# Adjacency tiles that serve two sweeps: a six-sweep graph kernel with the flat sweeps in alternating row order

## The reference

```
L0: inv_deg = 1/(adj.sum(1) + beta); x = LN(x + inv_deg * (adj @ x + beta*x) @ kernel + bias)
L1: h = relu(adj @ (x @ W1) + b1); h = relu(adj @ (h @ W2) + b2); h = relu(adj @ (h @ W3) + b3)
    x = LN(x + relu(h + x))          # W1: 128 x 20, W2: 20 x 20, W3: 20 x 128
L2: fc = x @ W + b; d = 1/(sqrt(adj.sum(1)) + 1e-8); x = LN(x + (adj * d[:,None] * d[None,:]) @ fc)
L3: S = (x@W_l) @ (x@W_r).T; x = LN(x + adj @ x + gamma * softmax(S) @ x @ W_h @ W_g)
```

## Time and profile before

| what | us |
|---|---|
| median of 3 runs | 1440.37 |
| profiled execution, its own time | 1445.9 |
| its span | 1444.3 |
| PE, DVE, ACT, GpSimd busy | 1367.3, 899.6, 709.5, 254.9 |
| copy of the last sum of sweeps 0, 3, 4, 5 starts at | 265.17, 634.50, 825.42, 1011.34 |
| HBM read | 342.65 MB |

### The profile page before, as it was taken

One profiled execution on the slowest core, in us unless ns is written; L12 is line 12 of the kernel. 1 busy time (PEld: TensorE's weight loads), 2 busy tenths in 40 slices (PEclk: granted clock), 3 DMA queues, 4 the chain that ended last, 5 costly groups with the idle time before them and its releaser, 6 DMA issues.

```text
span 1444.3 us, 17225 instructions
## 1 busy us (share of the span) xinstructions
PE 1367.3 (95%) x5879; PEld 798.7 (55%) x5879; DVE 899.6 (62%) x1194; ACT 709.5 (49%) x883; POOL 254.9 (18%) x167
## 2 busy tenths in 40 slices
PE   6999999888898999999999999999899999999987
PEld 2555555321222222247777778888667777767754
DVE  4676777300000013368888898888788888888885
ACT  1110011111101111257777787776787887887786
POOL 0111111000000000101010000000533333345345
PEclk9999999999999999999999999999999999999999
DMA  9866677699999999998999999997000000000000
GB/s 361 332 260 233 253 277 271 248 391 406 407 404 408 408 401 408 390 362 301 313 323 309 338 324 365 354 386 271 0 0 1 0 1 0 1 1 29 0 1 29
DMA packets 103455, 345.69 MB, mean 239 GB/s; under 512 B 11610, under 2 KB 13274, under 8 KB 103386
## 3 DMA queue, kind: packets, MB, share of 16 engines
q1 hardware_dynamic: 101136, 343.98, 63.3%
q10 hardware_dynamic: 2250, 0.82, 0.2%
HBM read 342.65 MB, written 2.10 MB: 239 GB/s over the span
## 4 chain that ended last, share of the span: by engine, by line
PE 75%; DMA 15%; DVE 5%; ACT 3%; issue 1%; POOL 0%; SPq 0%; DVEq 0%; ACTq 0%
DMA raw<-in_adj_s 15%; PE acc L1104 11%; PE acc L1140 9%; PE acc L1202 7%; PE acc L1197 7%; PE acc L1198 7%; PE acc L1297 6%; PE acc L1124 4%; PE acc L1227 2%; PE acc L1287 2%; PE acc L1291 2%; PE acc L1288 2%; DVE t_lo L829 2%; PE e L1252 2%; PE e L1254 2%; PE e L1253 2%
## 5 line engine op out<-in xcount | busy, mean ns | idle before, releaser
L829 DVE TENSOR_TENSOR t_lo<-raw,t_hi 128x1024 fp32r<-128x1024 f32 x240 | 292.1, 1248 | 42.4 <-ACT t_hi L589 36.9
L589 ACT ACTIVATE t_hi<-raw 128x1024 fp32r<-128x1024 f32 x240 | 251.5, 1058 | 60.4 <-PE acc L1202 58.9
L1197 PE MATMUL acc<-t_hi,st_hi 128*128 128x512 f32 x480 | 202.3, 421 | 2.9 <-DVE st_lo L734 2.9
L500 POOL TENSOR_TENSOR ring_lo<-ring,p_hi 128x1024 fp32r<-128x1024 f32 x64 | 155.6, 2430 | 220.2 <-ACT p_hi L647 220.1
L1198 PE MATMUL acc<-t_hi,st_lo 128*128 128x512 f32 x480 | 187.5, 391 | 0.0
L1140 PE MATMUL acc<-raw,h_a 128*20 128x512 f32 x736 | 161.8, 599 | 25.8 <-DMA raw<-in_adj_s 25.5
L1104 PE MATMUL acc<-raw,x 128*128 128x512 f32 x384 | 174.0, 608 | 11.2 <-DMA raw<-in_adj_s 11.2
L760 DVE TENSOR_TENSOR xs<-e,bias 128x512 f32<-128x512 f32 x8 | 5.5, 690 | 272.0 <-PE e L1020 272.0
L534 ACT ACTIVATE at<-acc 128x512 f32<-128x512 f32 x48 | 28.7, 598 | 266.4 <-PE acc L1140 181.9
L913 DVE TENSOR_TENSOR ring<-ring,e 128x1024 f32<-128x1024 f32 x128 | 154.1, 1212 | 0.7 <-PE e L1267 0.6
L1202 PE MATMUL acc<-t_lo,st_hi 128*128 128x512 f32 x480 | 149.9, 393 | 0.7 <-DVE t_lo L829 0.7
(11 more groups left out here) (189 smaller groups left out, 2062.1 us busy)
## 6 DMA issues: line engine op xcount, KB each, us to landing
raw<-in_adj_s SPq DMA_DIRECT2D x600, 512.0 KB, 6.9
resident<-in_adj_s SPq DMA_DIRECT2D x16, 512.0 KB, 7.7
raw<-in_adj_s SPq DMA_DIRECT2D x24, 256.0 KB, 7.7
kept_t<-in_adj_s SPq DMA_DIRECT2D x8, 512.0 KB, 5.8
x<-in_x SPq DMA_DIRECT2D x4, 512.0 KB, 8.4
kept_s<-in_adj_s SPq DMA_DIRECT2D x8, 256.0 KB, 6.1
kept_v<-in_adj_s SPq DMA_DIRECT2D x8, 256.0 KB, 6.5
kept_l<-in_adj_s SPq DMA_DIRECT2D x8, 256.0 KB, 9.0
```

Source lines behind the costliest of these rows:

```text
L500: nc.gpsimd.tensor_tensor(ring_lo[:, n % RING, :], slot(n), p_hi[:, m % 2, :].bitcast(F32), ALU.subtract).then_inc(pl_done, 1)
L589: nc.scalar.activation(t_hi[:, (par * wide_tiles(s) + g) % HL, :], raw[:, k, :], ACT.Copy).then_inc(hi_done, 1)
L829: nc.vector.tensor_tensor(t_lo[:, k, :], raw[:, slot_no(s, c, g), :], t_hi[:, k, :].bitcast(F32), ALU.subtract).then_inc(lo_done, 1)
L1197: mm(a[:, :], block_of(st_hi, b), hi[:, m], start=(b == 0), stop=False)
```

## The change

The flat sweeps are planned by a list of items (tile of row chunk c, column chunk d, half h). Sweeps 1 and 3 take the row chunks backwards (7 to 0). When tile (c, d) is on chip for sweep s and the `h` of sweep s+1 for column chunk d is already known, its product for sweep s+1 is added too, in a second accumulator `ahead` (the banks of `rs01`), and the tile is not needed in sweep s+1. ACT stores the partial sum (`store_ahead`, in `sums`), and in sweep s+1 DVE, not ACT, takes the chunk's sum and adds the stored one (`evacuate_narrow`). The distance in rows from which a tile is joined is `lag`: 1 in sweep 0, 2 in sweeps 1 and 2, and 1 in the rows c > 3 of sweep 2, which lets these last four chunks also join the column chunk next to them.

```
+ORDER = (tuple(range(NC)), tuple(reversed(range(NC))), tuple(range(NC)), tuple(reversed(range(NC))))
+LATE = 1
+KEPT = tuple((c, c + 1) if c + 1 < NC else (c, c - 1) for c in range(NC))
+def lag(s, c):
+    return 1 if s == 0 or s == 2 and c > 3 else 2
+def joined(s, c, d):
+    return s < 3 and used(s, c, d) and ORDER[s].index(c) - ORDER[s].index(d) >= lag(s, c)
+def used(s, c, d):
+    return s == 0 or not joined(s - 1, c, d)
+def held(s, c, d):
+    return d in KEPT[c] and not (s == 0 and c == LATE)
...
+def order_of(s, c):
+    mine = [d for d in range(NC) if used(s, c, d)]
+    if s == 0:
+        last = [d for d in mine if c > 0 and d in KEPT[c] and d != c - 1] + [d for d in mine if d == c - 1]
+    else:
+        last = [d for d in (c + 1, c - 1, c) if d in mine and d in KEPT[c]]
+        if s == 1:
+            mine.reverse()
+    return [d for d in mine if d not in last] + last
```

In sweep 0 (`first_sweep`) a joined column chunk gets its four narrow matmuls after its second tile; in `narrow_sweep` each joined tile has its own two blocks in two strips and the next sweep's two in the other two:

```
+                    if i.fused and i.h == 1:
+                        wait_h(pe, 0, i.d)
...
+                        for b in range(CB):
+                            t = tile_of(0, c, items[n - 1 + b // GB])
+                            m = mm(f[32 * b:32 * b + H, :], h_a[:, (i.d * CB + b) * H:(i.d * CB + b + 1) * H],
+                                   t[:, b % GB * CW:(b % GB + 1) * CW], start=(i.d == joint[0]),
+                                   stop=(i.d == joint[-1]))
...
+                    for j in range(GB):
+                        b, k = i.d * CB + i.h * GB + j, 32 * (2 * i.h + j)
+                        m = mm(a[k:k + H, :], h[:, b * H:(b + 1) * H], t[:, j * CW:(j + 1) * CW],
+                               start=(i.d == items[0].d), stop=(i.d == items[-1].d))
+                    if i.fused:
+                        for j in range(GB):
+                            b, k = i.d * CB + i.h * GB + j, 32 * (2 * (1 - i.h) + j)
+                            m = mm(f[k:k + H, :], h_next[:, b * H:(b + 1) * H], t[:, j * CW:(j + 1) * CW],
+                                   start=(i.d == joint[0]), stop=(i.d == joint[-1]))
```

```
+                    if n == (1 if r > 0 else -1):
+                        epilogue_1(ps, pr, pr % 2)
+                    if ps < 3 and (n == (min(4, len(items) - 1) if r > 0 else -1)):
+                        epilogue_2(ps, pr)
+                    if s == 3:
+                        for q in TURNED[r]:
+                            if n == (2 if q < r - 1 else 9):
+                                epilogue_3(3, q)
+                            if n == (4 if q < r - 1 else 12):
+                                epilogue_4(3, q)
```

with `TURNED[r]` the rows q whose turn belongs to row r: r - 2 for q up to 3, r - 1 for later ones. Before the first item of sweep 1 PE runs all of the last row's epilogue. On DVE a row of sweep 3 is, in order:

```
+                evacuate_narrow(ps, pr)
+                if ps == 3:
+                    residual_1(ps, pr)
+                    residual_2(ps, pr)
+                    statistics(ps, pr)
+                    scales(ps, pr)
+                    for q in TURNED[r]:
+                        laplacian_h(q)
+                    if r > 2:
+                        stationary_lo(S4, row(3, r - 3))
```

More of the change, by code:

```diff
@@ L23 @@
 NG = NB // GB
-RB = 4
 TW = GB * CW
@@ L62, with done, row, plan @@
 }
-def done(stage, s, c):
-    return c + (1 + NC * sum(q < s for q in STAGES[stage]))
+def done(stage, s, r):
+    return r + (1 + NC * sum(q < s for q in STAGES[stage]))
+ORDER = (tuple(range(NC)), tuple(reversed(range(NC))), tuple(range(NC)), tuple(reversed(range(NC))))
+LATE = 1
+KEPT = tuple((c, c + 1) if c + 1 < NC else (c, c - 1) for c in range(NC))
+Item = namedtuple("Item", "d h kept fused seq")
+def row(s, r):
+    return ORDER[s][r] if s in FLAT else r
+def lag(s, c):
[15 more added lines that the diff above has]
+    return [d for d in mine if d not in last] + last
+def plan():
+    items, seq = {}, 0
+    for s in FLAT:
+        for r, c in enumerate(ORDER[s]):
+            here = []
+            for d in order_of(s, c):
+                for h in range(CB // GB):
+                    streamed = not held(s, c, d)
+                    here.append(Item(d, h, not streamed, joined(s, c, d), seq if streamed else None))
+                    seq += streamed
+            items[s, r] = here
+    return items, seq
+ITEMS, T_WIDE = plan()
+STORES = [(s, r) for s in FLAT for r in range(NC) if any(i.fused for i in ITEMS[s, r])]
+def stored(s, c):
+    return STORES.index((s, ORDER[s].index(c))) + 1 if (s, ORDER[s].index(c)) in STORES else 0
+def same_bank(s, r):
+    return max((n + 1 for n, (q, t) in enumerate(STORES) if (q, t) < (s, r) and t % 2 == r % 2), default=0)
 def build(nc, adj_s, x_dram, beta_in, ident_in, comb_in, w, out):
@@ L392, in load_kept @@
             def load_kept(c):
[L393 to L407, removed]
-            def step(s, c, par):
[L410 to L422, removed]
+                if c > 2:
+                    sp.wait_ge(res_in, 64 * (c - 2))
@@ L423, in step @@
+            first_of_1 = min(i.seq for r in range(NC) for i in ITEMS[1, r] if not i.kept)
+            def step(s, c, par):
+                if s in FLAT:
+                    flat(s, c)
+                    return
+                for g in range(NG):
+                    wait_slot(sp, s, c, g)
                     k = slot_no(s, c, g)
[L424 removed]
+                    sp.dma_start(raw[:, k, :], tile(c, group_no(s, c, g))).then_inc(raw_in[k], 16)
@@ L534, in evacuate, with store_ahead @@
                 nc.scalar.activation(at[:, :], acc[par][:, :], ACT.Copy).then_inc(S["at"], 1)
+            def store_ahead(s, r):
+                if (s, r) not in STORES:
+                    return
+                act.wait_ge(pe_acc, s * NC + r + 1)
+                if s > 0:
+                    act.wait_ge(S["at"], done("at", s, r))
+                nc.scalar.activation(sums[:, row(s, r), :], ahead[r % 2], ACT.Copy).then_inc(sums_done, 1)
             def second(s, c):
```

542 lines of the change are left out of this document (293 added, 249 removed).

## The result

The changed kernel takes 1362.27 us (median of 4 runs, 1358.85 to 1367.14) against 1440.50 in the same set: ratio 0.946, interval 0.9425 to 0.9497. In a second set it was 1363.14 (0.9437 to 0.9476). The prediction was 1339 in a range of 1318 to 1372; the rival of longer chains stood at 1365. So the time lies in the stated range, but above the 1326 to 1355 that was given for the forecast itself, and nearest to the rival of longer chains, which had a chance of 0.17. The profiled execution took 1359.29 us with a span of 1357.5, and from here on it is compared with before's 1444.3.

A forecast was written before the change was run, and what follows sets the result against it. Sweeps 1 to 3 were taken to wait for adjacency tiles. Stages 297.2 + 237.6 + 189.2 + 185.9 + 433.0 = 1342.9 against a 1444.3 span, 101.4 less; from the 1440.4 median, 1339 us, range 1318 to 1372.

The forecast's parts named there:

- the rival of longer chains: Sweeps 1 to 3: longer hops in 24 rows, 14 us, slow PE in 12 rows, 12 us; 1365 us, chance 0.17.
- signs named for a wrong prediction: Joined tile over 1 us, joined column in sweep 0 over 1.3 us, or sweep 3 over 90 us.
- Price of a column on PE: Sweeps 1 and 2: a joined tile takes 0.86 us, an unjoined one 0.43; bounds for joined 0.86 and 3.44.
- both rivals with two accumulators: Joined tiles in sweeps 1 and 2: in pairs, 1418 us, chance 0.04; one after another, up to 1576 us, 0.03.
- Sweep 1: Starts with a 13.1 us chain, then PE is full; takes 81.6 us, before about 127.
- Sweep 3: Nothing joined; DVE's chain decides; PE ends at +74.5, with loading and low clock 79 us.
- Row 0: Sweep 0's first row: PE waits 7 us for bx, row ends at 45.8 instead of 44.8; bounds 40 and 48.
- Sweep 4: Later chunks 22.6 us each, PE 22.3 and DVE 21.9; whole sweep 189.2 us, before 190.9.
- Sweep 2: Starts with a 3.7 us chain, row 0 1.8, row 1 4.7; takes 77 us.
- near but under it: Sweep 2's loading: 46 tiles after +6.4 end at +68, within the sweep's 77 us.
- Sweep 4's first chunk: Takes 31 us from the end of sweep 3, waiting inside DVE for the w3 matmuls; bounds 28 and 35.
- Sweep 0: 28 joined columns at 1.1 us add 31 us on full PE; ends at 297.2, before 265.2.

The follow-up runs named there:

- the half loads: Changed kernel, but in sweep 3's rows 4 to 7 only the first column block of each streamed tile is loaded: 1361.54 us.
- Moving DVE's steps: Changed kernel with constants first, PE kept busy and lag 2 in sweep 2; DVE's epilogue steps one tile later in sweep 4's first chunk: 1347.97 us against 1345.64.
- PE kept busy: Changed kernel plus idle wide matmuls in PE's waits where sweeps 1, 2 and 3 begin: 1356.62 us, 6.5 less than the changed kernel.

## Why the prediction was right, and where it was short

The direction, the range and the cause hold: the loads of the narrow sweeps were the bound, and without joined tiles the kernel takes 24 us more than before. None of the signs named for a wrong prediction came (a joined tile 0.86 us, a joined column in sweep 0 1.18, sweep 3 81.4). These steps came out as worked out. *Price of a column on PE*: a joined tile is 0.86 us, so both rivals with two accumulators are gone. *Sweep 1*: 82.3 us for 81.6, its first sum 14.9 us after sweep 0's last (the forecast's chain of 13.1 and one column of 0.87 at half the clock make 14.8).

*Sweep 3* came out near its number in part by luck. Evacuations (DVE taking a finished sum) came at +5.2, 11.6, 20.1, 29.4, 38.7, 53.5 and 67.4 where 5.0, 11.5, 19.4, 27.9, 36.4, 49.5 and 62.6 stood. PE ended at +81.4, where the rows had been added up to +74.5 and 4.5 us put on top for loads and a low clock. The loads are worth 1 to 3 us by the half loads, and the low clock was in row 2 alone (0.57 from 480 to 484 us, about 1 us). So some 3 to 5 of the 6.9 us are hops longer than worked out (an estimate from these numbers), and the allowance hid part of them. DVE after, from the last scale of one row to the next row's sum:

```profile
512.67 0.16 DVE L933 SCALAR_TENSOR_TENSOR nmr<-mv,rstd 128x4 f32<-128x4 f32 x1
...
519.33 0.69 DVE L940 TENSOR_TENSOR v<-e,bias_l 128x512 f32<-128x512 f32 x1 [5.17 <-PE e L1223]
...
521.27 0.68 DVE L859 TENSOR_TENSOR at<-acc,sums 128x512 f32<-128x512 f32 x1
```

It waits 5.17 us for xn, turn, copy and weights, with nothing else in its list. Part of this is not the chain: xn was ready at 514.52 and PE turned it at 515.72, after tiles that came at the full traffic; the turned copy was ready at 517.01 and PE came to the weights at 518.13, after the three tiles that the hooks put between. The forecast's hops had neither of these two waits. The half loads took 1.1 us off the 5.17.

*Row 0* ended at 45.24 where 45.8 with the restart was forecast, but by luck: I had the copy of x as last, and it was beta's landing, 9 us after its issue. `bx` was ready 1.4 us later than forecast, and the rest of the row was 2.0 us shorter (2.2 for 4.2). *Sweep 4*: 22.3 us a chunk, not 22.6; DVE's 21.9 under PE's 22.3 was room enough.

The span of the profiled execution came 14.6 us over the forecast's 1342.9. The terms that were too small:
- Sweep 2, 9.1 us, the largest. 3.2 us are the low clock at its start: the sums of its rows 0 and 1 came 8.0 and 6.5 us after the ones before, and 5.6 and 5.7 in traces whose clock stayed up there. I had charged a low clock to sweep 1 and not here, since PE's single waits are under 1 us. Another 1 us a row in rows 1 to 3 I put down to a pair taken apart: the hook after item 4 stands between the two halves of a column that is not joined. No run moved the hook.

```profile
392.38 1.90 PE L1328 MATMUL acc<-kept_late,rsum 128*20 128x512 f32 x12
394.21 1.06 PE L1199 MATMUL e<-ident,xt 20*128 20x20 f32 x8
395.20 1.04 PE L1328 MATMUL acc<-kept_late,rsum 128*20 128x512 f32 x4
```

The last line is one tile in two strips, alone, and PE's next narrow record starts 0.87 us after it at the earliest for the same strips: 0.86 and not 0.43. I had halved the price of every unjoined tile. Most of the rest, 2.3 us, is in rows 6 and 7, where the DMA share was 1.03 and tiles came late:

```profile
464.08 0.61 PE L1328 MATMUL acc<-raw,rsum 128*20 128x512 f32 x2 [0.53 <-DMA raw<-in_adj_s]
```

The step "near but under it" compared sums over the whole sweep; in the short first rows the loads had stood still (DMA share 0.00 from 389 to 391 us), and that time was not to be had back.
- Sweep 4's first chunk, 3.2 us: its waits of PE for DVE and ACT add up to 6.0 us. Moving DVE's steps removed one and made another.
- Sweep 0, 2.2 us: 1.18 for 1.1 an insertion, and 0.8 in row 1, which began at the low clock after the wait for `bx`. The Trainium skill, "TensorEngine Tiling (Array Packing)", Key Properties, says that a change of tiling mode drains the engine. The 0.32 us a round agrees with it in kind.

The other 8.5 us of the 23 between 1339 and 1362.3 are not in any stage. I worked the saving out from a profiled execution 5.5 us above its median and took it off the median, and the profiled one after lies 3.0 us below its own. With nine runs that differ by 8 us, in step with their clock, a difference of two single executions has that error in it.

The rival of longer chains gave 1365, near the median by part of its mechanism. Of its 14 us for longer hops, spread over 24 rows, the trace shows those 3 to 5 in sweep 3 and almost none in sweep 1. Its other half, the low clock in 12 rows for 12 us, was real where sweeps begin, and is worth 6.5 us for the three starts.

Not settled: what makes the runs with PE kept busy still vary by 3.5 us, what moving sweep 2's hook would bring, and whether lag 1 in sweep 2's last rows is worth 1 us in either direction.

## What to carry to other kernels

When a tile on chip can serve two passes, count PE and the first rows as well as the bytes. Against the same order without joining, 75.5 MB less are 144 tiles, or 186 us at 1.29 us each, and the time fell by 102 us. Against the kernel before, the 132 tiles saved in the narrow sweeps (170 us) are 116 for the whole kernel, since sweep 4 loads 16 more, and the time fell by 78 us. A pass that begins with short rows turns each latency that the bulk had covered into time, and here the clock of PE went with it: look for windows at 1.2 GHz, and try filling the waits with matmuls into a bank about to be begun. Before believing the sum of a row, look at which halves of a pair stand on either side of a hook.

## What the hardware showed that was not expected

- Eleven unused matmuls in PE's waits paid: 6.5 us less, as the granted clock went from 0.50 to 1.00 in 303 to 315 and 385 to 391 us.
- The clock fell to 0.50 at 385 us after two PE waits of 0.83 and 0.77 us among other short gaps in sweep 2's start, and did not fall at the start of sweep 3 in the same execution, with waits of 0.83, 0.77 and 0.42. The same code gives either from run to run: the kernel with half loads has the same code up to row 4 of sweep 3, and at sweep 2's start its clock stayed up.

```profile
385.00:387.00 2.00, 1.23 (x9) 0.91 (x8) 0.00 (x0) 1.16 (x2) 0.00 (x0) 1.00 1.00 399
387.00:391.00 4.00, 4.00 (x32) 1.10 (x35) 0.69 (x1) 0.27 (x2) 0.00 (x0) 1.00 0.32 110
```

- The 16 KB of beta took 9 us to land when their load was issued at 32.4 us behind 17 small ones, with tiles still loading at a DMA share of 1.09 and 1.05 (32 to 40 us).
